# A graph attention layer: summing the high and the low part of V in one wide product for ten of 32 row tiles

## The reference

```python
h = jnp.maximum(_layernorm(x), 0.0)              # x: 4096 x 128
h = h @ W.T + b_W                                # inside the layer
e = (h @ a1)[:, None] + (h @ a2)[None, :] + b_a[0]
e = jnp.where(e > 0, e, 0.2 * e)
scores = jnp.where(adj > 0, e, -9e15)            # adj: 4096 x 4096 int32
return x + jax.nn.softmax(scores, axis=1) @ h
```

## Time and profile before

| what | value |
|---|---|
| median of 3 runs (lowest to highest) | 202.63 us (202.22 to 203.68) |
| profiled execution, its own time | 203.52 us |
| span of the profiled execution | 201.9 us |
| TensorE busy | 197.2 us, 98% |
| VectorE busy | 183.1 us, 91% |
| ScalarE busy | 147.9 us, 73% |
| GpSimd busy | 53.8 us, 27% |
| moved over the span | 375 GB/s on average |

### The profile page before, as it was taken

The page is one execution under the profiler, slowest core; times in us unless marked ns, Lnnn a source line. Parts: engine busy times, 40 slices in busy tenths (PEclk is TensorE's granted clock), DMA queues, the critical chain, the costliest instruction groups (busy, mean ns, idle before and its releaser), DMA issues.

```text
span 201.9 us, 7231 instructions
## 1 busy us (share of the span) xinstructions
PE 197.2 (98%) x3183; PEld 190.4 (94%) x3183; DVE 183.1 (91%) x265; ACT 147.9 (73%) x192; POOL 53.8 (27%) x66
## 2 busy tenths in 40 slices
PE   7989999999999999999999999999999999999994
PEld 7558888999999999999999999999999999999994
DVE  4679999999999899987999999989999999999845
ACT  2299988799872777779988688799688888985000
POOL 1000659689997011055000000061000000620000
DMA  5999999999999999999999999999999999996012
GB/s 174 367 412 420 404 411 422 425 406 380 427 428 415 417 424 419 417 425 411 422 419 420 417 417 425 414 420 419 415 419 422 420 414 422 420 356 208 7 38 71
DMA packets 15968, 75.66 MB, mean 375 GB/s; under 512 B 1600, under 2 KB 5952, under 8 KB 7616
## 3 DMA queue, kind: packets, MB, share of 16 engines
q1 hardware_dynamic: 15792, 75.06, 91.3%
q10 hardware_dynamic: 144, 0.13, 0.3%
HBM read 73.08 MB, written 2.11 MB: 372 GB/s over the span
## 4 chain that ended last, share of the span: by engine, by line
PE 97%; ACT 1%; issue 0%; DVE 0%; POOL 0%; POOLq 0%
PE ps L843 29%; PE ps L841 29%; PE ps L847 29%; PE ps L815 4%; PE ps L805 3%; PE ps L857 2%; ACT L411 1%; PE ps L883 1%; ACT hT L335 0%; PE ps L861 0%; PE ps L866 0%; DVE xT L542 0%; PE ps L860 0%; POOL ones L717 0%; ACT warm L411 0%
## 5 line engine op out<-in xcount | busy, mean ns | idle before, releaser
L841 PE MATMUL ps<-V,w 128*128 128x129 f16 x1024 | 174.3, 220 | 0.0
L843 PE MATMUL ps<-V,w 128*128 128x129 f16 x1024 | 174.3, 220 | 0.0
L847 PE MATMUL ps<-V,w 128*128 128x129 f16 x1024 | 174.3, 220 | 0.0
L379 ACT ACTIVATE mask<-adj_sb 128x1024 bf16<-128x1024 int32 x126 | 125.3, 1056 | 27.1 <-DMA adj_sb<-in_adj_t 27.1
L459 DVE SCALAR_TENSOR_TENSOR w<-g_row,pairs,mask 128x1024 f32<-128x1024 f32 x96 | 120.5, 1317 | 5.5 <-ACT mask L379 3.7
L841 PEld LDWEIGHTS ps<-V,w 128*128 128x128 f16 x1024 | 100.2, 98 | 1.5 <-ACT H L340 0.7
L843 PEld LDWEIGHTS ps<-V,w 128*128 128x128 f16 x1024 | 100.2, 98 | 1.0 <-issue 1.0
L847 PEld LDWEIGHTS ps<-V,w 128*128 128x128 f16 x1024 | 100.3, 98 | 0.0
L459 DVE SCALAR_TENSOR_TENSOR w<-ps,pairs,mask 128x1024 f32<-128x1024 f32 x31 | 37.4, 1265 | 0.0
L792 POOL TENSOR_TENSOR xT<-xT,x_sb 128x512 f32<-128x512 f32 x6 | 11.7, 1970 | 76.8 <-ACT xT L394 76.8
L815 PEld LDWEIGHTS ps<-wp,hT 128*128 128x128 f32 x64 | 8.0, 193 | 2.4 <-ACT hT L335 1.7
(11 more groups left out here) (93 smaller groups left out, 62.6 us busy)
## 6 DMA issues: line engine op xcount, KB each, us to landing
adj_sb<-in_adj_t SPq DMA_DIRECT2D x64, 1024.0 KB, 10.5
xT<-in_x_t SPq DMA_DIRECT2D x8, 256.0 KB, 7.2
x_sb<-in_x_p SPq DMA_DIRECT2D x3, 512.0 KB, 10.6
g_row<-g_dram SPq DMA_DIRECT2D x1, 1536.0 KB, 11.0
out<-xT SPq DMA_DIRECT2D x3, 512.0 KB, 9.9
x_sb<-in_x_p SPq DMA_DIRECT2D x2, 256.0 KB, 4.3
out<-xT SPq DMA_DIRECT2D x1, 192.0 KB, 2.0
out<-xT SPq DMA_DIRECT2D x3, 64.0 KB, 1.6
```

Source lines behind the costliest of these rows:

```text
L379: nc.scalar.activation(mask[:, m % MASKS, r], adj_sb[:, m % HELD, r], ACT.Relu, scale=CONNECTED).then_inc(mask_ready, 1)
L841: nc.tensor.matmul(sums[:, bank, a, :], w16[:, m % SLOTS, col:col + P, 1], V[:, jt, 0, 0:NF], start=(jt == 0 and a == 0), stop=False, skip ...
L843: nc.tensor.matmul(sums[:, bank, a, :], w16[:, m % SLOTS, col:col + P, 1], V[:, jt, 1, 0:NF], start=False, stop=False, skip_group_check=True)
L847: last = nc.tensor.matmul(sums[:, bank, a, :], w16[:, m % SLOTS, col:col + P, 0], V[:, jt, 0, 0:NF], start=False, stop=(jt == NT - 1), ski ...
```

## The change

V's denominators get a low part too: the high part of V now has 130 columns (128, the column factor in half precision, and what half precision leaves of it), the low part 128. A denominator is the sum of the two last columns. In ten row tiles (tile 6 of groups 0 and 2, tiles 0 to 4 of group 1, tiles 0, 2 and 4 of the last group) high weights multiply the high and the low part of V at once, in one product of 258 columns, and their sums lie apart in PSUM (`parted`). Low weights still multiply the 130 columns of the high part. The other 22 tiles have products of 130, 128 and 130 columns, of which the middle one adds to the first 128 columns.

PSUM is laid out anew: group 1 takes the banks 3 to 7, the last group's tiles lie two to a bank in banks 3 to 5. PIECES become (0, 2), (2, 4), (4, 6), (6, 7), (7, 8). ScalarE scales the low sums of the parted tiles into `extra` and GpSimd adds them to Z; in the last group VectorE adds them with one more instruction a tile. Denominators are added by reductions or, in the last group, by one instruction a tile that also multiplies by the norm, so that a reciprocal gives the factor. The reciprocal of `scores` into H is gone; a cast and a subtraction in `scale_weights` and `ones_low` take its place.

```diff
-    NF = DOUT + 1
-    VW = DOUT + 8
+    NF = DOUT + 2
+    LO = NF
+    VW = LO + DOUT + 6
+    MERGED = LO + DOUT
...
-    PIECES = ((0, 3), (3, 5), (5, 6), (6, 7), (7, 8))
+    PIECES = ((0, 2), (2, 4), (4, 6), (6, 7), (7, 8))
...
+        if group % 2 == 0:
+            return (k // 3, k % 3 * NF) if k < 6 else (2, (k - 6) * MERGED)
         if group < NG - 1:
-            return 3 * (group % 2) + k // 3, k % 3
-        return ((3, 0), (3, 1), (3, 2), (4, 0), (4, 1), (5, 0), (6, 0), (7, 0))[k]
+            return (3 + k, 0) if k < 5 else (k - 2, MERGED)
+        return ((3, 0), (3, MERGED), (4, 0), (4, MERGED), (5, 0), (5, MERGED), (6, 0), (7, 0))[k]
+
+    def parted(group, k):
+        if group % 2 == 0:
+            return k == 6
+        return k < 5 if group < NG - 1 else k in (0, 2, 4)
...
-        V = sb("V", [P, NT, 2, VW], F16)
+        V = sb("V", [P, NT, VW], F16)
...
-                        ins = nc.scalar.activation(Z[:, g, :], sums[:, bank, a, 0:DOUT], ACT.Copy, scale=rg[:, g:g + 1])
+                        ins = nc.scalar.activation(Z[:, g, :], high_sums(group, k)[:, 0:DOUT], ACT.Copy, scale=rg[:, g:g + 1])
+                        if parted(group, k):
+                            ins = nc.scalar.activation(extra[:, apart.index(g), :], low_sums(group, k), ACT.Copy,
+                                                       scale=rg[:, g:g + 1])
...
-                    nc.vector.reciprocal(rden[:, r], of).then_inc(rden_ready, 1)
...
+                    for k in range(k0, k1):
+                        of = high_sums(NG - 1, k)
+                        ins = nc.vector.tensor_scalar(den[:, first + k:first + k + 1], of[:, DOUT:DOUT + 1],
+                                                      of[:, DOUT + 1:NF], gg[:, 1:2], ALU.add, ALU.mult)
+                    ins.then_inc(sums_added, 1)
+                    dve.wait_ge(sums_added, NG - 1 + i + 1)
+                    nc.vector.reciprocal(rg[:, first + k0:first + k1], den[:, first + k0:first + k1]).then_inc(rg_ready, 1)
+                    if i == len(PIECES) - 1:
                         check_last()
...
+                    split = [k for k in range(*PIECES[i]) if parted(NG - 1, k)]
+                    for k in split:
+                        g = first + k
+                        nc.vector.scalar_tensor_tensor(Z[:, g, :], low_sums(NG - 1, k), rg[:, g:g + 1], x_sb[:, g, :],
+                                                       ALU.mult, ALU.add).then_inc(rows_begun, 1)
...
-                    nc.vector.reciprocal(H[:, r, ONE], rstd[:, 2, r]).then_inc(ones_ready, 1)
...
+                    nc.vector.tensor_copy(V[:, r, DOUT], ev[:, r]).then_inc(ones_begun, 1)
+
+                def ones_low(part):
+                    r = slice(*PARTS[part])
+                    dve.wait_ge(ones_begun, part + 1)
+                    nc.vector.tensor_tensor(V[:, r, DOUT + 1], ev[:, r], V[:, r, DOUT], ALU.subtract
+                                            ).then_inc(ones_ready, 1)
...
+                    if k0 == 0 and m in FIRST_OF_PART:
+                        pe.wait_ge(ones_ready, FIRST_OF_PART.index(m) + 1)
...
-                            nc.tensor.matmul(sums[:, bank, a, :], w16[:, m % SLOTS, col:col + P, 1], V[:, jt, 0, 0:NF],
-                                             start=(jt == 0 and a == 0), stop=False, skip_group_check=True)
-                            nc.tensor.matmul(sums[:, bank, a, :], w16[:, m % SLOTS, col:col + P, 1], V[:, jt, 1, 0:NF],
-                                             start=False, stop=False, skip_group_check=True)
-                            last = nc.tensor.matmul(sums[:, bank, a, :], w16[:, m % SLOTS, col:col + P, 0], V[:, jt, 0, 0:NF],
+                            first = jt == 0 and sums_at(group, k)[1] == 0
+                            if parted(group, k):
+                                nc.tensor.matmul(both_sums(group, k), w16[:, m % SLOTS, col:col + P, 1], V[:, jt, 0:MERGED],
+                                                 start=first, stop=(jt == NT - 1), skip_group_check=True)
+                            else:
+                                nc.tensor.matmul(high_sums(group, k), w16[:, m % SLOTS, col:col + P, 1], V[:, jt, 0:NF],
+                                                 start=first, stop=False, skip_group_check=True)
+                                nc.tensor.matmul(low_sums(group, k), w16[:, m % SLOTS, col:col + P, 1],
+                                                 V[:, jt, LO:LO + DOUT], start=False, stop=False, skip_group_check=True)
+                            last = nc.tensor.matmul(high_sums(group, k), w16[:, m % SLOTS, col:col + P, 0], V[:, jt, 0:NF],
                                                     start=False, stop=(jt == NT - 1), skip_group_check=True)
...
                     if m == PAIRS:
                         pe.wait_ge(h_ready, NCH)
+                        pe.wait_ge(w_ready, 2 * PAIRS)
```

More of the change, by code:

```diff
@@ L81, in gat_layer_kernel @@
     PARTS = ((0, GI), (GI, 2 * GI), (2 * GI, NT))
+    FIRST_OF_PART = tuple(first // 2 for first, _ in PARTS)
     FIRST_SETS = 2
-    PIECES = ((0, 3), (3, 5), (5, 6), (6, 7), (7, 8))
+    PIECES = ((0, 2), (2, 4), (4, 6), (6, 7), (7, 8))
     ENDS = 3
@@ L94, in sums_at @@
     def sums_at(group, k):
+        if group % 2 == 0:
+            return (k // 3, k % 3 * NF) if k < 6 else (2, (k - 6) * MERGED)
         if group < NG - 1:
-            return 3 * (group % 2) + k // 3, k % 3
-        return ((3, 0), (3, 1), (3, 2), (4, 0), (4, 1), (5, 0), (6, 0), (7, 0))[k]
+            return (3 + k, 0) if k < 5 else (k - 2, MERGED)
[4 more added lines that the diff above has]
+        return k < 5 if group < NG - 1 else k in (0, 2, 4)
+    apart = [GI * group + k for group in range(NG - 1) for k in range(GI) if parted(group, k)]
     with ExitStack() as ctx:
@@ L135, in gat_layer_kernel @@
         st = sb("st", [P, NT, 2], F32)
+        extra = sb("extra", [P, len(apart), DOUT], F32)
         eg = sb("eg", [P, 2, NT], F32)
@@ L162, in gat_layer_kernel, with high_sums, low_sums, both_sums @@
         Z = xT[:].rearrange("p (g d) -> p g d", d=DIN)
-        sums = ps[:, :, 0:3 * NF].rearrange("p b (a n) -> p b a n", a=3)
+        def high_sums(group, k):
+            bank, at = sums_at(group, k)
+            return ps[:, bank, at:at + NF]
+        def low_sums(group, k):
+            bank, at = sums_at(group, k)
+            at += LO if parted(group, k) else 0
+            return ps[:, bank, at:at + DOUT]
+        def both_sums(group, k):
+            bank, at = sums_at(group, k)
+            return ps[:, bank, at:at + MERGED]
         w16 = w[:, :, :].rearrange("p a n -> p (a n)").bitcast(F16).rearrange("p (a n h) -> p a n h", a=SLOTS, h=2)
@@ L538, in rows @@
                     dve.wait_ge(xb_ready, len(SETS))
-                    for k in range(*PIECES[i]):
[L540 to L543, removed]
+                    first = GI * (NG - 1)
+                    split = [k for k in range(*PIECES[i]) if parted(NG - 1, k)]
[3 more added lines that the diff above has]
+                                                       ALU.mult, ALU.add).then_inc(rows_begun, 1)
+                    for k in range(*PIECES[i]):
+                        if k not in split:
+                            g = first + k
+                            ins = nc.vector.scalar_tensor_tensor(Z[:, g, :], high_sums(NG - 1, k)[:, 0:DOUT], rg[:, g:g + 1],
+                                                                 x_sb[:, g, :], ALU.mult, ALU.add)
+                    for k in split:
+                        g = first + k
+                        dve.wait_ge(rows_begun, sum(parted(NG - 1, n) for n in range(k + 1)))
+                        ins = nc.vector.scalar_tensor_tensor(Z[:, g, :], high_sums(NG - 1, k)[:, 0:DOUT], rg[:, g:g + 1],
+                                                             Z[:, g, :], ALU.mult, ALU.add)
                     ins.then_inc(rows_ready, 1)
@@ L791, in _ @@
                     pool.wait_ge(scaled_rows, r + 1)
-                    nc.gpsimd.tensor_tensor(Z[:, k, :], Z[:, k, :], x_sb[:, k, :], ALU.add).then_inc(rows_added, 1)
+                    ins = nc.gpsimd.tensor_tensor(Z[:, k, :], Z[:, k, :], x_sb[:, k, :], ALU.add)
+                    parts = [g for g in apart if k.start <= g < k.stop]
+                    if parts:
+                        step(ins)
+                        e = apart.index(parts[0])
+                        ins = nc.gpsimd.tensor_tensor(Z[:, parts[0]:parts[-1] + 1, :], Z[:, parts[0]:parts[-1] + 1, :],
+                                                      extra[:, e:e + len(parts), :], ALU.add)
+                    ins.then_inc(rows_added, 1)
                 pool.wait_ge(bad_ready, 4)
```

69 lines of the change are left out of this document (33 added, 36 removed).

## The result

The changed kernel takes 206.49 us (median of 4 runs, 206.25 to 207.67), the kernel before 202.43 on the same chip (4 runs, 201.84 to 203.68). The ratio is 1.0202, interval 1.0149 to 1.0256: 4.06 us slower, where 1.06 us less was forecast, and outside the range. The profiled execution of the changed kernel took 207.67 us around a span of 206.0.

The account below looks back on a forecast made before the run. TensorE's gapless products were taken to bound the kernel. Products -1.66 us, start +0.1 and end +0.5 sum to -1.06 us, from the median 202.63 to 201.6 us; range 201.0 to 203.3.

Parts of the forecast that it names:

- What bounds the kernel: TensorE's products run without a gap from first to last; a cycle saved per product shortens the end, later work adds whole.
- The end: VectorE's work after the last products, recut into 2, 2, 2, 1, 1 tiles: 0.5 us more, bounds 0.1 and 0.7.
- The products: TensorE's 704 plain triples 0.59 us less, 320 merged ones 1.07 us less: together 1.66 us less.
- c = 6: Fixed part of each TensorE product taken as 6 cycles on even widths, giving 1.65 us less over all triples.
- The start at byte 260: TensorE's read of V's low part 260 bytes into a row: named as possibly slower than others, given no size.
- Supply of weights: Extra work on ScalarE, GpSimd and VectorE delaying weights for TensorE: costed at nothing, bounds 0 to 0.3 us.
- the cover of 0.62 us: At pair 7, weights ready at 43.25 us for a product at 43.87; forecast no stall there.
- The 0.1 us that it put on the start: VectorE's low-part instructions for the first denominators, ahead of the first weigh: 0.1 us more, bounds 0 and 0.4.
- weight loads set the floor: Rival: weight load, not columns, spaces narrow products; plain triples stay at 408 cycles, merged 400; 202.2 us, chance 0.2.
- the fixed part is 7 or 8: Rival: larger fixed cycles per product, products 0.51 us less at 7 or 0.64 more at 8; chance 0.2 for slower.
- a product of 258 columns is issued as two: Rival: merged triples stay three products, 202.6 us; chance within the 0.05 for the rest (no merging, stalls).
- merging takes away all of the fixed part: Rival: in the ten merged tiles all of the fixed part goes, needed for a faster verdict; chance 0.05.

## Why the prediction was wrong, point by point

**What bounds the kernel** was right: the products run without a gap behind pair 7, and whatever comes after the last one is added whole.

**The end** is the step that failed. It followed the last product to the last store and the flag, took the later of the two as the end, and passed over the 1.86 us from the flag to the end of the span (200.04 to 201.9) as if they could not change. The branch over the general path is in that stretch, and its 0.47 us became 3.47. Three runs show that it turns on where the branch and its target lie in the program: the changed kernel gets fast by instructions that do nothing, and the kernel before gets slow by them, or by instructions that never run. The trace of the kernel before has a row of the branch; that its price can change by seven times no row of that trace showed.

Within the part that was costed the size was off: 0.88 us for 0.5, over its bound of 0.7. The order of events was as told (VectorE waits for the third piece and never after). Counted from the third piece's first sum, the reciprocal came at 0.51 us for 0.34, the last piece's sum at 2.64 for 2.46, the last check at 3.03 for 2.80. The mis-sized term is the first: two sums were put 0.09 apart, like two small instructions of the earlier trace rows, and 0.25 to what needs them; they took 0.20 apart, and 0.31 to the reciprocal. And VectorE then stood 0.6 us late at the last piece instead of 0.42. The 0.5 was also a middle between 0.40 for the last row and 0.66 for the last check, and it is the check that counts, as the branch follows the flag at the same 1.06 us in both kernels.

**The products** were right in their count and wrong in their sum. The sum is in cycles, 408 for the 170.0 ns of three products; no run shows a cycle or how many of them a product takes. What the runs show in its place is nanoseconds: once the low part starts at byte 0, 128, 130 and 258 columns take 55.84, 56.67 and 110.00 ns. By the last two a column more adds 0.417 ns, and each of the three stands 2.5 ns above its columns, 6.0 times that, so c = 6 holds in this measure and the forecast of -1.66 us with it. The start at byte 260, left unpriced, made it -0.21: 1.45 us of the 5.1 by which the forecast missed.

**Supply of weights.** Costed at nothing with 0.3 as a bound: 0.17 at pair 7, in the bound. That it came out so near was in part luck. The prediction priced the low parts of the first and of the third part of the denominators, not of the second, and by the timeline above it was mostly the second part's cast and subtraction that used up the cover of 0.62 us. The 0.1 us that it put on the start can't be told from the scatter of the first product.

**The rivals.** That weight loads set the floor falls: with the low part first 128 columns are spaced 55.84 ns, 130 columns 56.67. That the fixed part is 7 or 8, on which the chance of 0.2 for slower and the range's upper end of 203.3 rest, falls with the same numbers, so the forecast's sign was lost by no rival that was named. That a product of 258 columns is issued as two falls by its 110 ns. That merging takes away all of the fixed part falls too: a merged triple takes 166.67 ns, where its 388 columns alone, at the 0.417 ns measured for one, would be 161.7.

**What the change is worth** without the two accidents: nothing measurable, 1.0000 (0.9974 to 1.0025). Unmerged in the last group it may be 0.4 us, 0.9980 (0.9960 to 1.0001), which these runs cannot tell from nothing.

## What to carry to other kernels

Follow the trace to the end of the span, past the last useful instruction: a branch over a path that is not needed cost about 0.5 or 3.5 us here by its place alone, and 142 to 144 instructions more ahead of it took 3.0 us from one kernel and added 3.4 to the other, so a verdict on such a change needs a look at the branch first. Lay out what TensorE reads so that each read starts at a multiple of 16 bytes, the starts that were fast here (55.8 ns a product of 128 columns at bytes 0 and 272, 59.5 and 59.6 at 264 and 260), and check the distance of starts of each product by itself, as a mean over tiles hides which of them lost. When an order of work is tight at its end, count each dependent step of the new order by the row of an instruction that reads what the new one reads.

## What the runs showed of the hardware

- TensorE's branch took 0.38 to 0.49 us where no block of instructions was loaded during it, and 3.44 to 3.83 us where one of 16384 bytes was, 0.9 to 1.0 us after the branch's start (twelve traces).
- A half precision product of 128 columns took 55.8 ns to the next start when its data started at bytes 0 or 272 of the row, 59.5 and 59.6 at 264 and 260.
- 129 columns cost what 130 do: 170.0 ns for three of either.
- A subtraction of eight columns on VectorE took 1.05 us at 27.82 us, until 0.05 us after a GpSimd instruction of 1.04 us had ended, and 0.19 us at 16.51 us, with GpSimd at rest.
